# Another order of the work on every engine of an attention and slot-mixture kernel, and a last batch like the others

## What is computed

```python
# x: (32, 256, 128)
# first half: causal linear attention with 16 heads of 8
q, k, v = heads(ln(x) @ Wq.T + bq), heads(ln(x) @ Wk.T + bk), heads(ln(x) @ Wv.T + bv)
q, k = exp(q), exp(k)
kv = cumsum(k[..., :, None] * v[..., None, :], axis=tokens)
k1 = cumsum(k, axis=tokens)
att = einsum('zsD,zsDd->zsd', q, kv) / sum(q * k1, axis=-1)
x = x + ln(att @ Wo.T + bo)
# second half: soft mixture of 512 slots, per batch
xn = rms_norm(ln(x), gamma_x); se = rms_norm(slot_embeds, gamma_slot)
logits = xn @ se.T                        # 256 x 512
dispatch = softmax(logits, axis=tokens); combine = softmax(logits, axis=slots)
slots = dispatch.T @ xn                   # 512 x 128
processed = gelu(slots @ w1) @ w2         # w1: 128 x 512, w2: 512 x 128
x = x + ln(combine @ processed)
```

## Time and profile before

| what | value |
|---|---|
| runs | 635.28 us median of 3 (634.94 to 636.53) |
| profiled execution, first to last instruction (span) | 633.3 us; its time with what lies around it isn't listed apart |
| busy share PE, weight loads, DVE, ACT, POOL | 92%, 81%, 75%, 69%, 76% |
| granted TensorE clock, mean | 0.996 of full |

### The profile page before, as it was taken

One profiled execution on the slowest core, in us unless ns is written; L12 is line 12 of the kernel. 1 busy time (PEld: TensorE's weight loads), 2 busy tenths in 40 slices (PEclk: granted clock), 3 DMA queues, 4 the chain that ended last, 5 costly groups with the idle time before them and its releaser, 6 DMA issues.

```text
span 633.3 us, 11705 instructions
## 1 busy us (share of the span) xinstructions
PE 583.9 (92%) x4136; PEld 515.1 (81%) x4136; DVE 475.3 (75%) x922; ACT 438.2 (69%) x1087; POOL 481.5 (76%) x495
## 2 busy tenths in 40 slices
PE   3456999999999999999999999999999999999886
PEld 2344888888898888888988888898988888888875
DVE  5978687887777788877777888777778788767521
ACT  4135677777777777777777777777777777777755
POOL 5878788888888888888888888888888888873100
PEclk9999999999999999999999999999999999999999
DMA  3000001000000000000000000000000000000000
GB/s 100 17 18 18 18 9 33 10 26 26 26 26 26 21 22 16 21 26 25 26 26 26 18 18 18 26 26 26 26 26 19 25 9 26 18 18 9 9 9 18
DMA packets 16829, 14.35 MB, mean 23 GB/s; under 512 B 2850, under 2 KB 16644, under 8 KB 16772
## 3 DMA queue, kind: packets, MB, share of 16 engines
q1 hardware_dynamic: 14708, 12.76, 6.7%
q10 hardware_dynamic: 2064, 0.86, 0.5%
HBM read 5.25 MB, written 4.19 MB: 15 GB/s over the span
## 4 chain that ended last, share of the span: by engine, by line
PE 51%; DVE 23%; ACT 18%; issue 4%; POOL 2%; DMA 1%; SPq 0%; DVEq 0%; POOLq 0%; ACTq 0%
PE HB L912 16%; DVE WB L1170 12%; PE LA L889 9%; ACT L477 6%; PE LA L868 5%; ACT comb L597 5%; PE WB L750 3%; PE WB L840 3%; ACT slT_hi L474 2%; PE LB L878 2%; DVE xnT_lo L1127 2%; DVE att L1180 2%; PE WB L791 2%; ACT xnT_hi L474 2%; PE WB L824 2%
## 5 line engine op out<-in xcount | busy, mean ns | idle before, releaser
L912 PE MATMUL HB<-w_c,hid 128*128 128x128 f32 x992 | 120.7, 275 | 0.5 <-ACT hid L481 0.5
L912 PEld LDWEIGHTS HB<-w_c,hid 128*128 128x128 f32 x992 | 117.3, 192 | 0.7 <-ACT hid L481 0.7
L481 ACT ACTIVATE hid<-HB 128x512 f32<-128x512 f32 x128 | 76.6, 599 | 32.1 <-PE HB L752 26.1
L1155 DVE TENSOR_TENSOR prod<-WB,E 128x768 f32<-128x768 f32 x96 | 90.9, 948 | 5.3 <-PE WB L841 5.1
L214 POOL TENSOR_TENSOR kv<-E 128x1024 f32<-128x1024 f32 x32 | 68.4, 2136 | 33.4 <-ACT E L474 33.4
L1170 DVE TENSOR_REDUCE WB<-prod 128x288 f32<-128x2304 f32 x32 | 81.9, 2561 | 3.1
L338 POOL TENSOR_TENSOR kv_lo<-kv,kv_hi 128x1152 fp32r<-128x1152 f32 x31 | 82.3, 2656 | 2.5
L398 POOL TENSOR_TENSOR kv<-kv,kv_prev 128x1024 f32<-128x1024 f32 x31 | 74.1, 2390 | 0.0
L214 POOL TENSOR_TENSOR kv_prev<-prev 128x1024 f32<-128x1024 f32 x31 | 66.2, 2136 | 2.6 <-DMA prev<-E 2.6
L925 PE MATMUL LA<-proc,comb 128*128 128x129 f32 x512 | 62.6, 274 | 1.5 <-ACT proc L474 1.5
L889 PE MATMUL LA<-xn,disp 128*128 128x129 f32 x512 | 62.6, 275 | 0.5 <-ACT disp L474 0.4
(11 more groups left out here) (143 smaller groups left out, 1517.9 us busy)
## 6 DMA issues: line engine op xcount, KB each, us to landing
X<-in_L_attn_x_dram SPq DMA_DIRECT2D x32, 128.0 KB, 2.2
out_dram<-res SPq DMA_DIRECT2D x32, 128.0 KB, 1.8
prev<-E SPq DMA_DIRECT2D x32, 112.0 KB, 2.1
w_in<-in_L_ffn_w_dram ACTq DMA_DIRECT2D x2, 256.0 KB, 4.5
prev<-E SPq DMA_DIRECT2D x32, 15.0 KB, 2.0
se_in<-n_L_ffn_slot_embeds_dram ACTq DMA_DIRECT2D x1, 256.0 KB, 3.6
w_in<-in_L_attn_Wq_dram SPq DMA_DIRECT2D x1, 64.0 KB, 2.2
w_in<-in_L_attn_Wk_dram SPq DMA_DIRECT2D x1, 64.0 KB, 2.2
```

The costliest lines, as they stand in the source:

```text
L481: act.activation(hid[:, f, :], HB[:, f % 2, :], ACT.Gelu).then_inc(gelu_ready[f], 1)
L912: last = pe.matmul(PR[:, j, :], hid[:, f, j * P:(j + 1) * P], w2_c[:, f, :], start=(f == 0), stop=(f == FJ - 1))
L1155: dve.tensor_tensor(prod[u][:, :, d0 * DIM:d1 * DIM].rearrange("p c (d f) -> p c d f", d=g), WB[:, k % 2, 0:g * DIM].rearrange("p (o d f) ...
```

## The change

Every engine's list is in another order, and the waits follow from it (a wait that another one implies is left out). The forms of the last batch are gone. `project`, `hidden`, `dispatch_transpose`, `combine_exp` and the eviction of q, k and v are functions of one piece each now, so that pieces can stand apart. The first 6 to 9 steps and the last few are written out batch by batch, in an order that differs a little from the loop's; the loop is `for s in range(9, 30)` or near. The instructions of a batch are the same. The diff, cut to the loops:

```diff
 POOL
-            def step(z, a, b, l, r, t, p, q, w):
-                    own_product(t, t % 2)
-                    pair_sum(t)
-                    own_value(r, r % 2)
-                    sums_high(t)
-                    sums_low(t)
-                    o_rstd_of(a)
-                    outer_even(p, p % 2)
-                    x_rstd_of(q)
-                    y_rstd_of(r)
-                    outer_odd(p, p % 2)
-                    x1_rstd_of(r)
+            def step(s):
+                x_rstd_of(s)
+                own_product(s - 1)
+                x1_rstd_of(s - 3)
+                outer_even(s - 1)
+                outer_odd(s - 1)
+                pair_keys(s - 1)
+                pair_sum(s - 1)
+                o_rstd_of(s - 5)
+                x_negative(s - 1)
+                sums_high(s - 1)
+                sums_low(s - 1)
+                own_value(s - 1)
+                y_rstd_of(s - 2)
...
             def own_product(n):
-                after(pool, own_den, n - 1)
+                if n in (3, 4):
+                    after(pool, own_den, n - 1)
 PE (before: p is s, t is s - 1, r is s - 2, l is s - 3, b is s - 4, and a is s - 5)
-                    mixture(a, a % 2)
-                    xn_transpose(l)
-                    hidden(b)
-                    x_transpose(p)
-                    logits(l)
-                    att_transpose(r)
-                    project(p)
-                    process(b, (2, 3))
-                    part_transpose(l)
-                    attention_out(r)
-                    cumulate(t, 0)
-                    dispatch_transpose(l)
-                    process(b, (0, 1))
-                    gather_slots(l)
-                    cumulate(t, 1)
-                    subtract_max(l)
-                    cumulate(t, 2)
-                    slots_transpose(l)
+                x_transpose(s)
+                hidden(s - 4, 1)
+                hidden(s - 4, 0)
+                logits(s - 3)
+                hidden(s - 4, 3)
+                att_transpose(s - 2)
+                hidden(s - 4, 2)
+                project(s, 0)
+                project(s, 1)
+                process(s - 4, 0)
+                part_transpose(s - 3)
+                attention_out(s - 2)
+                cumulate(s - 1, 0)
+                dispatch_transpose(s - 3, 0)
+                dispatch_transpose(s - 3, 1)
+                process(s - 4, 1)
+                cumulate(s - 1, 1)
+                gather_slots(s - 3)
+                cumulate(s - 1, 2)
+                xn_transpose(s - 2)
+                subtract_max(s - 3)
+                slots_transpose(s - 3)
+                mixture(s - 4)
 DVE, the new step
+                x_statistics(s)
+                second_residual(s - 6)
+                token_maxima(s - 4)
+                first_residual(s - 3)
+                multiply(s - 2, 0)
+                x_normalise(s)
+                multiply(s - 2, 1)
+                x1_normalise(s - 3)
+                slots_scale(s - 4)
+                multiply(s - 2, 2)
+                xnT_low(s - 3)
+                slT_low(s - 4)
+                attention_sums(s - 2)
+                attention(s - 2)
+                xT_low(s)
+                part_maxima(s - 3)
+                slot_maxima(s - 3)
+                own_sum(s - 1)
 SP
-                    store(b, b % 2)
-                    load(t + NX)
-                    shift_odd(w, w % 2)
+                load(s)
+                store(s - 8)
+                shift_odd(s - 1)
...
             def shift_odd(n):
-                after(sp, v_copied, n)
+                if n in (1, 3, 6):
+                    sp.wait_ge(v_copied, n + 1)
 the last batch
-                    if n == NB - 1 and f > 1:
-                        process_last(f - 2)
...
-                        for f in range(FJ - 2, FJ):
-                            process_last(f)
```

More of the change, by code:

```diff
@@ L187, in attention_and_slot_mixture @@
[L187 to L192, removed]
+        dispT_done = [sem(f"s_dispT{k}") for k in range(NC)]
@@ new lines, in first_steps @@
+                process(1, 0)
+                part_transpose(2)
+                attention_out(3)
+                cumulate(4, 0)
+                dispatch_transpose(2, 0)
+                dispatch_transpose(2, 1)
+                process(1, 1)
+                cumulate(4, 1)
+                gather_slots(2)
+                xn_transpose(3)
+                subtract_max(2)
+                cumulate(4, 2)
+                slots_transpose(2)
+                mixture(1)
+                x_transpose(6)
@@ new lines, in first_steps @@
+                hidden(2, 1)
+                hidden(2, 0)
+                logits(3)
+                hidden(2, 3)
+                att_transpose(4)
+                hidden(2, 2)
+                project(6, 0)
+                project(6, 1)
+                process(2, 0)
+                part_transpose(3)
+                attention_out(4)
+                cumulate(5, 0)
+                dispatch_transpose(3, 0)
+                dispatch_transpose(3, 1)
+                process(2, 1)
+                cumulate(5, 1)
@@ new lines, in first_steps @@
+                gather_slots(3)
+                cumulate(5, 2)
+                xn_transpose(4)
+                subtract_max(3)
+                slots_transpose(3)
+                mixture(2)
+                x_transpose(7)
+                hidden(3, 1)
+                hidden(3, 0)
+                logits(4)
+                hidden(3, 3)
+                att_transpose(5)
+                hidden(3, 2)
+                project(7, 0)
+                project(7, 1)
+                process(3, 0)
@@ new lines, in first_steps @@
+                part_transpose(4)
+                attention_out(5)
+                cumulate(6, 0)
+                dispatch_transpose(4, 1)
+                dispatch_transpose(4, 0)
+                process(3, 1)
+                cumulate(6, 1)
+                gather_slots(4)
+                xn_transpose(5)
+                cumulate(6, 2)
+                subtract_max(4)
+                slots_transpose(4)
+                mixture(3)
+                x_transpose(8)
+                hidden(4, 1)
@@ new lines, in first_steps, with step @@
+                xn_transpose(6)
+                cumulate(7, 2)
+                subtract_max(5)
+                slots_transpose(5)
+                mixture(4)
+            def step(s):
+                x_transpose(s)
[21 more added lines that the diff above has]
+                mixture(s - 4)
```

1610 lines of the change are left out of this document (1023 added, 587 removed).

## The result

The changed kernel takes **743.61 us** (median of 4 runs, 734.38 to 745.77), the kernel before beside it 635.54 us (634.94 to 636.53). Two of the four executions, the profiled one among them, lie over 1.5% above the fastest and are left out of the ratio, 1.161 (738.06 against 635.54, 95% interval 1.155 to 1.167); by the median of all four it would be 1.170. The profiled execution took 745.48 us, its span is 743.7 us. I had said 702 us and a range up to 735: the direction came out, the size did not.

A forecast was written before the change was run, and what follows sets the result against it. The prediction took a 17.98 us batch chain, with PE nearly its bound; 27 batches at +2.3 us (62), fill +3 and tail +2 made +67 on 633.3, 700, plus 2 around the span: 702 us, range 645 to 735.

The forecast's parts named there:

- The hold: Steady batches: POOL's outer_even and outer_odd each hold one x1_normalise instruction on DVE; 20.3 us a batch, 2.3 more.
- A: Rival: x1_normalise runs unheld at 0.34 us an instruction and the new order wins; 626 us, chance 0.18.
- B: Rival: only x1_normalise's first instruction is held, the second slips in ahead of outer_odd; step 18.4, 652 us, chance 0.09.
- The step laid out: All engines' durations in one steady batch, laid from x_transpose: 17.45 us without holds, 20.3 us with both.
- The edits' own gain: Steady batches: reordering PE, ACT and POOL without any hold takes 17.45 us a batch, 0.53 less.
- rival C: PE's gap before xn_transpose also halves its clock: +1.7 a batch, 748 us if in all, 720 if 4 of 10; chance 0.13.
- The fill: Batches 0 to 2, bound by POOL's chain of sums, one instruction already held in two of three: +3 us.
- The tail: After the last Gelu all of process is left, but a table load and the split mixture go: +2 us.
- The SP edit: The two shift DMAs wait only for the exponentials, issue moves under 0.3 us; costed at nothing, 2 us without cover.
- The sum: Whole kernel: 62 us from 27 steady batches, +3 first batches, +2 end; +67 on 633.3 us, 702 us forecast.

The follow-up runs named there:

- e1: Changed kernel with POOL's outer_even and outer_odd also waiting for xn of two batches back; 624.65 us, ratio 0.983 to the kernel before.
- e5: Changed kernel with x1_normalise in the tensor_scalar form that also writes out an accumulator, values may differ, no wait added; 625.7 us, ratio 0.984.
- e7: Changed kernel where only outer_odd waits for xn of two batches back and outer_even runs on; 664.21 us, ratio 1.044.
- e2: Kernel before with two qk_own buffers, so POOL's own_product waits for own_sum of two batches back; 684.53 us, ratio 1.077.
- e3: Changed kernel with ten matmuls nobody reads put ahead of PE's xn_transpose from batch 2 on; 716.33 us, ratio 1.128.

## Why the prediction was off, point by point

**The hold: right.** Both instructions of x1_normalise are held, by outer_even and outer_odd, each to POOL's end, and xn_transpose, ahead of the slots and the mixture in PE's list, hands that on. e1, e5 and e7 take it away by a wait, by a form and by half; e2 makes it in the kernel before. Rivals A and B fell: xn is not at 0.34, and not in every second instruction. 55 of the 64 took over 1 us. B's price, 18.4 us, was measured in e7 as 18.77.

**The step laid out: 0.3 us short.** Forecast 20.3, measured 20.59; without hold forecast 17.45, measured 17.56. The term is the start of outer_even: I had x1_rstd done at 12.83 us of the step, it ends at 330.36 - 317.25 = 13.1. y_rs stands where I put it (9.67 for 9.7) and qk_own too; then x_vf waits 0.23 us for the squares of x1, which come out at 12.0 instead of 11.75. The chain of ACT and DVE through x1 was laid too tight. Over 28 intervals that is 8 us. The edits' own gain, forecast 0.53 a batch, is 0.42.

**The clock: this is the step that failed.** The sum has no term for it: I set rival C at 0.13 and left its upper part out of the range with the words "PE is busy for 17 us on both sides of the gap". It was so, and the clock fell all the same, 17 times in 28 intervals: 29.6 us of the profiled execution, 27.3 by the medians (e3). Without that loss the kernel takes 716.33 us, inside the range. C's price came out near, 1.7 us a fall against 29.6 / 17 = 1.74 measured, but that is luck in part: by C's own words (slots transposes of 0.47 us and a mixture of 1.80 twice as long) it would be 2.3, and nothing shows where 1.7 is from. Luck, too, is how close the result lies to the 748 us that C gives for a fall in every batch: there were fewer falls, and the fill and the step made up for them. What was wrong is C's chance and its place outside the sum. The gap of 2.65 us in the fill of before was followed by a fall. I argued it away by a difference between the two places that no row priced. The page "TensorE: Matmul & The Clock Gate" of the Trainium skill, part 1, has an idle array fall back to 1.2 GHz. The rows agree in that each of the 17 falls begins in a gap or up to 1.6 us behind one. A fall for every gap, as I drew from it, they don't show: of the 26 intervals with a gap of 2 us or more, 9 have none.

**The fill: +3 forecast, with bounds of -2 and +6, +9.8 measured.** I counted one held instruction as already paid in two of three batches and took the sums on POOL for the bound. Timeline of DVE in the fill of the changed kernel:

```profile
26.22 3.70 DVE L1423 TENSOR_SCALAR xh<-X,x_mv,x_rs 128x128 f32<-128x128 f32 x2
...
43.81 4.22 DVE L1564 TENSOR_SCALAR xn<-x,x_mv,x_rs 128x128 f32<-128x128 f32 x2
47.95 2.79 DVE L1423 TENSOR_SCALAR xh<-X,x_mv,x_rs 128x128 f32<-128x128 f32 x2
...
65.36 2.78 DVE L1423 TENSOR_SCALAR xh<-X,x_mv,x_rs 128x128 f32<-128x128 f32 x2
68.06 2.43 DVE L1564 TENSOR_SCALAR xn<-x,x_mv,x_rs 128x128 f32<-128x128 f32 x2
```

xh has the same form as xn and is held as well; behind a held xn it comes later and meets the next long instruction of POOL. In e1 the xn of 43.73 takes 0.60 us, and the reduce of batch 1 starts at 47.88 instead of 51.98. The xh of 26.22 is held in e1 as well and is no part of the difference. I priced the hold for xn in steady batches and forgot it in the fill.

**The tail: +2 forecast, -0.2 measured**, inside its bounds of 0 and +4. The SP edit, costed at nothing, stayed so: neither outer product waits for prev in the steady rows above.

**The sum.** Forecast +67: 62 for the step, 3 for the fill, 2 for the tail. Measured +110.4 in the profiled execution: 71.2 for the step, 29.6 for the clock, 9.8 for the fill, -0.2 for the tail. Two thirds of the miss is the clock, the rest is the fill and 0.3 us a batch.

**What stays open.** Why two batches of four keep the clock behind the same gap of 2.85 to 2.88 us isn't told by any row. The runs of the changed kernel spread by 11 us, and the fastest has the highest mean clock: 734.38 us at 0.959, 741.74 at 0.948, 745.48 and 745.77 at 0.947 and 0.946. But a lower mean is not lost time everywhere: of seven executions of the kernel before, beside e1 to e3, four at 0.970 to 0.973 took 634.66 to 635.51 us and three at 0.995 to 0.997 took 633.42 to 638.92. No trace shows where in those four the clock was down. What is left of the holds of xh in e1's fill (3.69 us at 26.14) was not tried on its own.

## What to carry to other kernels

A wait between DVE and POOL may be there by accident and still keep a short DVE instruction off a long POOL one; before taking it away, look at what POOL runs while DVE's tensor_scalars from SBUF to SBUF run, at 0.34 us free and 2.1 us held. If POOL has idle time later in its step, give the order back with a wait (e1); it made the new order 1.7% faster than the kernel before instead of 16% slower. A form of the DVE instruction that isn't held does the same for the time (e5, 1.6%), but only where its values are the ones wanted, which here they were not. And where a forecast opens a gap of some 3 us in an engine list of TensorE, price the clock as a term of the sum, not as a remote rival.

## What the runs showed of the hardware that I had not expected

- POOL's next instruction wins each time: kv_prev starts at 332.42, 0.04 us before the end of kv, and the second xn is held a full 2.1 us more. Where kv_prev waits for xn (e7) it starts 0.48 us behind the end of kv and the second is free; how short a pause would do isn't shown.
- Who starts first doesn't settle who is held: in the fill of the kernel before an xn instruction that starts 0.07 us ahead of POOL's is held for 2.27 us, in e2 one that starts 0.20 us ahead is not.
- The form of tensor_scalar with the accumulator costs 0.403 us for 128 columns against 0.340, plus reading the accumulator (0.08 us, beside the next), and takes no part in the hold.
- The clock fell behind gaps of 2.84 to 2.88 us, in some batches and not in others, and did not fall in the steady batches of e2 and e7 with their gaps of 0.97 and 1.05 us. The length of the gap alone doesn't decide: e7 has one fall in the loop, behind a gap of 2.05 us, and none behind two others of 2.06 and 2.07.
- Ten useless matmuls, twenty passes in the trace, per batch (2.39 us of PE in e3) made a kernel 27 us faster.
